# An expert block's raw load, rank matmuls, PSUM pairs and last token rows, placed anew in a two-layer attention kernel

## What is computed

```python
x = x + xattn0(layernorm(x), ctx)   # 16 heads of 16, bias -0.1*|tq-tk|, output projection
x = x + ffn0(layernorm(x))          # dense 1024-wide silu block + 4 heads x top 8 of 1024 small experts
x = x + xattn1(layernorm(x), ctx)   # 16 heads, relu(q Wq), relu(k Wk), relu(v Wv), no output projection
x = x + moe(layernorm(x))           # below

def moe(x):                         # 2048 tokens, E=8 experts, 2 of them for each token
    rn = (xf - mean) * rsqrt(var + eps) * gamma + beta
    probs = softmax(rn @ gate_w.T); rw, sel = top_k(probs, 2)
    h = gelu(einsum('nc,efc->enf', xf, w1)); y = einsum('enf,ecf->enc', h, w2)
    return einsum('enc,ne->nc', y, comb)     # comb: rw at the two chosen experts
```

## Time and profile before

| | us |
|---|---|
| three runs | 1123.56, 1125.65, 1127.57 |
| median | 1125.65 |
| profiled execution | 1118.98 |
| its span (first to last instruction) | 1116.8 |
| PE busy in it | 994.8 (89%) |
| DVE busy | 799.0 (72%) |
| ACT busy | 652.5 (58%) |
| POOL busy | 497.9 (45%) |
| mean granted clock of PE | 0.963 |

### The profile page before, as it was taken

One profiled execution on the slowest core, in us unless ns is written; L12 is line 12 of the kernel. 1 busy time (PEld: TensorE's weight loads), 2 busy tenths in 40 slices (PEclk: granted clock), 3 DMA queues, 4 the chain that ended last, 5 costly groups with the idle time before them and its releaser, 6 DMA issues.

```text
span 1116.8 us, 17009 instructions
## 1 busy us (share of the span) xinstructions
PE 994.8 (89%) x5550; PEld 632.4 (57%) x5550; DVE 799.0 (72%) x1755; ACT 652.5 (58%) x874; POOL 497.9 (45%) x550
## 2 busy tenths in 40 slices
PE   8889999989778989989999788899998887999991
PEld 3345344434457878778877563344443333888881
DVE  7767688887889798798987446788888844444443
ACT  4357667666566866777777524576675650455550
POOL 6558897896415435335434422215061634222220
PEclk9899999999999999999999989999999988999996
DMA  7855979648999500000003231465644247222226
GB/s 247 239 167 159 291 206 346 196 153 270 235 224 221 117 1 1 0 2 1 1 29 79 75 65 57 123 209 142 172 133 129 83 149 284 61 69 74 70 59 225
DMA packets 74200, 149.87 MB, mean 134 GB/s; under 512 B 7823, under 2 KB 44577, under 8 KB 72580
## 3 DMA queue, kind: packets, MB, share of 16 engines
q1 hardware_dynamic: 61380, 98.80, 33.8%
q0 software_dynamic: 10800, 47.63, 12.0%
q10 hardware_dynamic: 1936, 2.36, 0.6%
HBM read 73.14 MB, written 76.25 MB: 134 GB/s over the span
## 4 chain that ended last, share of the span: by engine, by line
PE 63%; DVE 16%; ACT 9%; issue 4%; POOL 4%; DMA 3%; SPq 1%; ACTq 0%; DVEq 0%; POOLq 0%
PE ps L1318 16%; PE ps L1452 10%; PE ps L1433 7%; PE ps L1418 5%; PE ps L1392 4%; PE ps L1402 4%; PE ps L1660 3%; PE ps L1637 3%; ACT pt L1105 3%; PE ps L1623 3%; DVE negmax L1859 2%; PE ps L1461 2%; PE ps L1783 1%; DVE moe_w L2205 1%; PE ps L1336 1%
## 5 line engine op out<-in xcount | busy, mean ns | idle before, releaser
L1859 DVE TENSOR_REDUCE negmax<-ps 128x2 f32<-128x1024 f32 x256 | 309.6, 1222 | 56.6 <-PE ps L1418 54.1
L1105 ACT ACTIVATE pt<-ps 128x1024 f32<-128x1024 f32 x256 | 259.2, 1027 | 136.1 <-PE ps L1433 134.5
L1452 PE MATMUL ps<-pt,v_aug 128*32 128x512 f32 x1024 | 143.1, 621 | 4.5 <-POOL pt L804 3.6
L1433 PE MATMUL ps<-sq,sk 57*128 57x512 f32 (+1 forms) x512 | 127.5, 496 | 6.0 <-DMA sq<-m_sb 3.5
L1418 PE MATMUL ps<-sk,sq 56*128 56x512 f32 (+1 forms) x512 | 107.8, 424 | 21.2 <-ACT pt L1105 16.1
L804 POOL TENSOR_TENSOR pt<-pt,near 128x256 f32<-128x256 f32 x128 | 92.4, 730 | 49.1 <-ACT pt L1105 48.4
L1433 PEld LDWEIGHTS ps<-sq,sk 57*128 57x128 f32 (+1 forms) x512 | 48.5, 186 | 105.7 <-issue 70.7
L996 POOL DMA_INDIRECT expert_out<-yo,dest x39 | 38.1, 976 | 117.4 <-ACT yo L1285 102.6
L908 POOL TENSOR_TENSOR w_first<-w_first,moe_w 128x1024 f32<-128x1024 f32 x16 | 38.1, 2383 | 106.4 <-DVE pt L2197 105.7
L1623 PE MATMUL ps<-sel,hl 128*128 128x512 f32 x256 | 73.4, 422 | 13.3 <-DVE pt L2197 13.3
L1418 PEld LDWEIGHTS ps<-sk,sq 56*128 56x128 f32 (+1 forms) x512 | 49.4, 190 | 42.4 <-ACT pt L1105 27.9
(11 more groups left out here) (323 smaller groups left out, 2083.6 us busy)
## 6 DMA issues: line engine op xcount, KB each, us to landing
expert_rows<-zero SPq DMA_DIRECT2D x3, 5586.0 KB, 61.4
expert_weights_split<-wst POOLq DMA_DIRECT2D x8, 2048.0 KB, 8.7
qk_rows<-hl SPq DMA_DIRECT2D x30, 512.0 KB, 3.1
sk<-qk_rows SPq DMA_DIRECT2D x62, 192.0 KB, 5.1
sq<-qk_rows SPq DMA_DIRECT2D x62, 192.0 KB, 4.5
moe_w<-in_w POOLq DMA_DIRECT2D x16, 512.0 KB, 7.7
wexp<-expert_weights_split POOLq DMA_DIRECT2D x16, 512.0 KB, 4.9
wexp<-expert_weights_split SPq DMA_DIRECT2D x4, 2048.0 KB, 16.4
```

The lines of the kernel that those rows point to most:

```text
L1105: act.activation(pt[:, 4 * (U % 2) + 2 * half:4 * (U % 2) + 2 * half + 2, :], ps[:, bank:bank + 2, :], ACT.Exp, scale=(BIAS, SCALE)[L]).th ...
L1433: ins = pe.matmul(ps[:, key.bank + s, :], sk[r, pair, c * P:(c + 1) * P], sq[r, pair, :], start=True, stop=True)
L1452: ins = pe.matmul(ps[32 * j:32 * j + 32, OBANK, :], v_aug[:, b % 2, c, HG * g + j, :], pt[:, 4 * (U % 2) + j, :], start=(c == 0), stop=(c ...
L1859: dve.tensor_reduce(negmax[:, n % 2, col:col + 9:8], ps[:, job.bank:job.bank + 2, :], AX, ALU.max, negate=True).then_inc(s_jd, 1)
```

## The change

Five pieces, all in one kernel:

1. `LOAD_RAW`: the raw weights of expert 2 are issued at step 10 instead of 15.
2. `ROUTE`: the rank job of batches 0 to 2 stands one step later (32 for 31), where it comes behind the second score half and the first values group. In `gate_pick` `pick16` is computed ahead of the two `pay` copies, for all batches.
3. `LATE`: in layer 0's steps 60 to 63 the score halves have fixed pairs, (2,3) and (4,5), and the jobs nt(1) and nx(1) take banks 0 and 1 instead of 7. The rotation stands still for the halves.
4. Last batch: its normalised rows are written by ACT, four activations with the root as scale and a new column `nb3` (minus mean times root) as bias, at step 78, instead of by POOL's `norm3`. Its statistics are taken in two pieces: 192 columns at step 64, the last 64 once the last residual is added. `gate_weights` comes one part earlier, ahead of the placing of tokens.
5. SP loads experts 4 and 5 as before; experts 6 and 7 in quarters of 512 KB, two ahead of each of the tile loads 3 to 6 (tile j's load is issued while tile j-3 runs). It reads the first row number before it waits for the sent rows. PE's `keep_busy(14)` becomes `keep_busy(12)`, a wait for all sent rows, and `keep_busy(2)`.

```diff
+LATE = 60
+LATE_BANKS = {("nt", 1): 0, ("nx", 1): 1}
-ROUTE = whole({23: ("gt", 0), 24: ("gt", 1), 25: ("gl", 0), 31: ("rk", 0)})
+ROUTE = whole({23: ("gt", 0), 24: ("gt", 1), 25: ("gl", 0), 32: ("rk", 0)})
-LOAD_RAW = (15, 16, 22, 28, 34, 40)
+LOAD_RAW = (10, 16, 22, 28, 34, 40)
@@ attention_jobs
+            elif (kind, i) in LATE_BANKS:
+                banks = (LATE_BANKS[kind, i],)
-            banks = next_pair()
+            banks = next_pair() if L or U < LATE else (2 + 2 * half, 3 + 2 * half)
@@ SP
-            for e in range(4, ME):
+            def last_expert(e, parts):
+                n = EW // 4
+                at_e = (ME - 1 - e) * EW
+                for i in parts:
+                    sp.dma_start(wexp[:, at_e + i * n:at_e + (i + 1) * n].bitcast(F32), wx[e, :, i * n:(i + 1) * n]).then_inc(s_wx[e], 16)
+
+            for e in (4, 5):
                 sp.dma_start(wexp[:, (ME - 1 - e) * EW:(ME - e) * EW].bitcast(F32), wx[e]).then_inc(s_wx[e], 16)
             sp.wait_ge(s_tile, 1)
-            for i in range(2):
-                sp.wait_ge(s_sent[i], 16 * 2 * TT * 2)
             for j in range(NTILE):
                 row = sp.value_load(tile_row[0:1, j:j + 1], min_val=0, max_val=XROWS - P)
+                if j == 0:
+                    for i in range(2):
+                        sp.wait_ge(s_sent[i], 16 * 2 * TT * 2)
+                if 3 <= j < 7:
+                    last_expert(6 + (j - 3) // 2, range(2) if j % 2 else range(2, 4))
@@ POOL
                 if b == B - 1:
-                    norm3(b)
                     send_rows(b, range(TT))
@@ ACT
+                    if L == 1 and U == LASTU + 14:
+                        act.wait_ge(s_nb, 1)
+                        act.wait_ge(s_sent[(B - 1) % 2], 16 * 2 * TT)
+                        for t in range(TT):
+                            act.activation(pay[:, (B - 1) % 2, t, 0:D], x_tok[:, B - 1, t, :], ACT.Identity,
+                                           bias=nb3[:, t:t + 1], scale=rs3[:, 0, t:t + 1]).then_inc(s_ln3, 1)
@@ PE
-            keep_busy(14)
+            keep_busy(12)
+            for i in range(2):
+                pe.wait_ge(s_sent[i], 16 * 2 * TT * 2)
+            keep_busy(2)
@@ DVE
+                    if L == 1 and U == LASTU:
+                        dve.wait_ge(s_res, NG * B - 1)
+                        stats_of(0, 64 * (NG - 1), 0, range(TT))
...
-                        if part == 12:
+                        if part == (11 if b == B - 1 else 12):
                             gate_weights(b)
@@ gate_pick
+                own.wait()
+                dve.tensor_tensor(pick16[:], pick[:, 0], pick[:, 1], ALU.add).then_inc(s_pick, 1)
+                if b == B - 1:
+                    dve.scalar_tensor_tensor(out=nb3[:], in0=mv3[:, :, 0], scalar=-1.0, in1=rs3[:, 0, :], op0=ALU.mult, op1=ALU.mult).then_inc(s_nb, 1)
                 if b >= 2:
                     dve.wait_ge(s_sent[b % 2], 16 * 2 * TT)
                 own(dve.tensor_copy(pay[:, b % 2, :, D + ME + 1], two_e[:, 0, :]))
                 own(dve.tensor_copy(pay[:, b % 2, :, D + ME], col("token")[:, TT * b:TT * (b + 1)]))
-                own.wait()
-                dve.tensor_tensor(pick16[:], pick[:, 0], pick[:, 1], ALU.add).then_inc(s_pick, 1)
```

More of the change, by code:

```diff
@@ L2050, in first_norm, with stats_of @@
                                       ALU.subtract, ALU.mult).then_inc(s_ln0, 1)
+            def stats_of(c0, c1, piece, blocks):
+                for t in blocks:
+                    own(dve.bn_stats(last6[:, t, piece, :], x_tok[:, B - 1, t, c0:c1]))
             def ln3_variance(b):
```

19 lines of the change are left out of this document (15 added, 4 removed).

## The result

The changed kernel takes 1118.91 us in the median of nine runs (1113.84 to 1121.16) against 1127.57 for nine runs of the kernel before: a ratio of 0.9925, 95% interval 0.9897 to 0.9953, or 8.5 us less, 5.3 to 11.6 by the interval. Scaled to the 1125.65 on which the prediction stood this is 1117.2; the forecast was 1114 with a range of 1107 to 1121, faster by more than 0.3%. The direction was right and the time inside the range, but the sum was some 3 us too good, and some terms are off by 1 us and more, in both directions. Two of the nine times of before, 1142.95 and 1145.39, lie far above the rest; without them its median is 1125.65 and the medians are 6.7 apart, still inside the interval.

What follows compares the result with a forecast made beforehand. The prediction took PE, busy 89% of the span, as the bound, with low clock following its stalls. Its terms -3.5 - 4.1 + 1.0 - 2.5 - 0.7 - 0.8 - 1.0 gave -11.6 us, 1114 from 1125.65, range 1107 to 1121.

Steps and rivals of the forecast that it cites:

- Raw load: Expert 2's load issued at step 10: the waits at its cast and PE's values go, -3.5 us (-5.5 to -2.0).
- P: Load at step 10 flows beside the stack loads: 2.7 us gained at step 20, about 1.4 lost at 14, net -1.3.
- Ranks: Rank jobs of batches 0 to 2: PE's waits are covered, -2.2, -0.5 and -1.4, together -4.1 us (-5.8 to -2.2).
- Fixed pairs: Layer 0, steps 60 to 63: nt(1)'s wait goes, a new wait for DVE comes at step 63, +1.0 us (-2.5 to +2.0).
- Last batch and first tile: Batch 2's wait -1.4, clock -2.5, DVE order -0.7, row number read early -0.8, first tile's clock -1.0 us.
- the bound of 4.3: Last batch at full clock: fillers, gate product, `keep_busy(3)` and transposes give at most 4.3 us; -2.5 was taken.
- The norm's "0": Last batch: POOL's norm ended ahead of the first send, so it was hidden and moving it to ACT gains 0.
- Expert quarters: Tile stage: two quarters take 2.1 us, a tile lasts 3.75, so the loads cost 0 (0 to +2).
- rival D: Tile stage: a tile load stands behind the quarters in SP's queue, slower, 1126 to 1138 us; chance 0.04.
- Rival A: Layer 0's late steps: the pairs gain what nt(1)'s wait shows, -2.5 for +1.0, 1110.5 us; chance 0.20.
- B: Last batch or first tile: the clock does not come back, -2.5 and -1.0 become 0, 1117.5 us; chance 0.20.
- C: Batch 1 and the pairs: DVE swallows what PE gets back, 1122.3 us and up, middle 1123; chance 0.07.

Runs made afterwards that it cites:

- the raw load alone: The kernel before with only expert 2's raw load moved from step 15 to 10; 0.9961 (0.9929 to 0.9993) of the kernel before.
- the ranks alone: The kernel before with only the ranks one step later and `pick16` ahead of the `pay` copies; 0.9949 (0.9917 to 0.9981) of the kernel before.

## Why the prediction was right, and where not

**Raw load, forecast -3.5 (-5.5 to -2.0).** The mechanism was right: step 19 to 20 is 2.2 to 2.9 shorter than in the trace of before in all ten traces with the load at 10. The step that failed is "I count them at nothing", said of the two issues and their company: in the same ten, steps 6 to 14 are longer by 0 to 1.4 in nine (and 5.3 once, with low clock), while the four traces with the load at 15 agree within 0.02 there.

What was left out is the load itself, which now flows beside the loads of the stacks. In five of the ten PE waits 0.4 to 1.1 for `sk` at step 14, and steps 6 to 14 are longer by that wait and 0.3; a sixth, with low clock, waits 1.96. All ten wait for `sq` twice, 0.2 to 1.0 some 4 us behind the exponential of step 19 and 0.7 to 1.4 some 20 us behind it; the four traces with the load at 15 have none of these waits. Whether the load delays these two, or PE only comes for the stacks 2.5 us sooner, no run tells.

The three stretches (6 to 14, 19 to 20, 20 to 30) take 80.2 us in the mean of the four and 78.5 in that of the ten: -1.7, outside the stated range; by the medians (80.2 and 78.0) it is -2.2, inside it. Of the two theories P is nearer, but its wait at step 14 is missing in four of the ten, the raw load alone among them, so that price is not fixed.

**Ranks, forecast -4.1.** Batch 0: the stall and its low clock gave 2.4 up to step 33, where 2.2 was taken, but over half of it was gone 14 steps later in eight of nine traces. The step that failed is "the wait is covered" taken as gain of the whole: DVE was not asked what it does with a PE that is early, though that was the argument for batch 1. Batch 1: -1.07 in all ten traces that move it, forecast -0.5; DVE swallowed less than feared. Batch 2: in the next term.

**Fixed pairs, forecast +1.0 (-2.5 to +2.0).** The new wait came where the order showed it, for the reason given, and the price against ten traces without it is +1.0, against the one trace of before +2.12, a little past the upper end; the clock at that place alone moves a trace by 2.7. The wait was 4.47 where 3.4 was worked out, and the low clock came with it, at a mean of 0.83 from step 60 to the first hidden product.

**Last batch and first tile, forecast -6.4 with batch 2's wait (-1.4 - 2.5 - 0.7 - 0.8 - 1.0), measured -6.33.** Right as a sum by errors that cancel. Counted from step 63's first exponential, the last rank job starts 6.0 us sooner (14.87 for 20.85), where 1.4 + 2.5 was forecast; the ranks alone give all of it (14.86). This is the term that was mis-sized most. The wait of 1.59 was worth 2.8 at the start of `keep_busy(2)`, since the values and the `ot` behind it had run slowly too; the four fillers gave 1.5 and the gate product 1.15, as in the bound of 4.3. The hold of 1.1 by `keep_busy(3)` mostly stayed: the clock fell to 0.62 behind the gate product, its six fillers took 4.52 for 5.02, and the rank job still starts 0.7 behind `pick16` (1.0 before).

The row numbers were forecast 0.7 earlier by the order on DVE and gained nothing in the changed kernel: they stand 2.54 behind the start of the rank job, for 2.13 before. The weights' operations, moved ahead of `place`, met the idle of 1.09 and 0.46 shown above, whose releaser is DVE's own operation ahead of it. Four of the ten traces with that order have it (0.9 to 1.1 and 0.5); five of the others have the row numbers 1.51 to 1.58 behind, the 0.6 that the term had meant. What makes DVE stand there stays open. The tile load goes out 0.9 sooner after the sends, 0.8 forecast. Then the split filler at half clock gave back 1.3 at the first transpose, as its bound of +0.9 had said it might, and the tile itself ran 1.0 faster.

The norm's "0" failed: it was hidden only as long as the row numbers were late, by 3.4 us of slack against a gain of 6. The text saw this ("if the row numbers came over 1 us sooner") and priced it at 0.1 to 0.5, for the norm on ACT; with the norm left on POOL the first send waits 2.5 and 3.9 us behind the row numbers instead of 0.9. Of the Trainium skill's rule (SBUF — State Buffer, Who interferes with whom) the traces say this: the difference of 0.54 takes 0.22 after, with the norm on ACT; it took 0.53 or 0.54 in the three traces in which POOL's norm ran beside it and 0.19 to 0.22 in the eleven others. So the rule agrees, for a price of 0.3 once.

**Expert quarters, forecast 0.** Right in time, not in size. "Two quarters take 2.1 us" failed: the first four land in 3.9 to 7.4 us after their issue. The tile loads behind them are held: in the six traces that give every landing, the fourth to the eighth take 2.1 to 6.0 us, in the trace of before 2.1 to 2.3. But they are held for 3.9 us at most, by the prediction's reckoning it costs from 5.4, and PE waits for no DMA in the tiles. So rival D's mechanism is there and its price is not. **Rival A** fell with the pairs' wait. **B** fell at the last batch, with the clock of 1.00; at the first tile the fillers ahead of it did run at half clock, and the tile itself at 0.90. **C** fell in its main point, though it was DVE that stood where batch 0's gain went in the changed kernel.

**Not in the sum at all:** the shift of SBUF, +0.9 at the end (26.3 in the mean of four traces, 25.4 in that of ten). It is in the diff, as two lines of declarations, and I read them as free.

Put together from the measured terms: -1.7 - 0.7 - 1.1 + 1.0 - 6.3 + 0.9 = -7.9, against -8.5 (-11.6 to -5.3) by the runs. The agreement is partly luck: the -6.3 is the difference of two traces and is -6.2 to -7.9 in the five others with the same last batch, and stretches that nothing in the change touches moved by 1 to 3 us from trace to trace.

## What to carry to other kernels

A wait removed is worth what the next steps leave of it, 14 of them here; follow the same instruction through to the next point where the engines meet before counting it. When one engine's chain gets shorter by several microseconds, redo the slack of everything that was called hidden behind it. And compare short stretches over several traces, not spans of two: here single executions differed by more than the whole change.

## What the runs showed of the hardware

- A tensor of 224 bytes declared early, which nothing uses, slowed 512 KB reads into SBUF from one per 1.36 us to one per 1.50 (some 385 and 349 GB/s in the view of DMA), and cost 0.9 us in the trace.
- The clock falls to 1.2 GHz not only after waits: PE was busy for 5.00 of 5.00 us at 1.00, and the 29 us after that ran at 0.53 with PE busy for 27.39 of them. And behind the same wait of 2.5 us at nt(1) the mean clock up to the first hidden product was 0.91 in five traces, 0.75 in four and 1.00 in one. The changed kernel's own runs spread by 7 us, the quick ones at 0.967 and the long ones at 0.958 and 0.959.
- DVE stood idle for 1.6 to 1.7 us at the same instruction of layer 1 in four of fourteen traces, on a wait whose releaser is not in the program.
